# Second expert stage: rows that carry their gates and weights, results added into the output by GpSimd's scatter

## The chip, the cores and the metric

The kernel runs on one core of a Trainium2 chip. The metric is the device time of one execution in microseconds (us), the median of several runs. The engines are named as the profile names them: PE (TensorE matmuls), PEld (its weight loads), DVE (VectorE), ACT (ScalarE), POOL (GpSimd), and SP, which here only issues DMAs.

## The reference, cut to what matters

Two layers follow each other; each is a gated attention and a gated mixture of experts over 4 x 512 tokens of 128 numbers. The change lies in the last part, the experts of layer 1, where every token goes to 2 of 8 experts:

```python
h = _layernorm(x, axis=-1) * (1 + cb) + sb
# _L1_ffn_ref, with x = h as 2048 rows of 128
routing_probs = jax.nn.softmax(x @ gate_w.T, axis=-1)
top_w, top_i = jax.lax.top_k(routing_probs, 2)
top_w = top_w / jnp.sum(top_w, axis=-1, keepdims=True)
gates = jnp.zeros((T, 8)).at[rows, top_i].set(top_w)
out = 0
for e in range(8):
    hid = jax.nn.silu(x @ w1[e].T) * (x @ w3[e].T)      # 448 wide
    out = out + hid @ w2[e].T * gates[:, e:e + 1]
x = x_before + gb * out                                  # gb: one row of 128 for each of the 4 batches
```

## The kernel before

Each engine has a program of its own, written out by hand and executed in order; semaphores join them. `Router` picks the experts and sorts the tokens: it counts how many tokens each expert has, gives each expert as many tiles of 128 rows as it needs (39 tiles for two choices per token), and computes for each tile a column of row numbers, `source` (which token each row is) and `home` (where its result goes). `sources` (L289 to L308) does the last of this on DVE.

`rows_out` (L410) writes the normalised rows to `h_rows` in DRAM, one DMA a batch, on SP. `experts_programs` (L896) then holds the programs of the five engines for the tiles:

- POOL gathers the 128 rows of a tile from `h_rows` into one of four buffers `f_hg` (L978), four tiles ahead, and scatters the results `f_y` of a tile to `back_rows` (L984). A token has two results, each with a row of its own in `back_rows`, and no scatter waits for another. In the loop of POOL, `gather(s + 4)` stands ahead of `scatter(s - 2)`.
- PE transposes the gathered tile (L1154), multiplies it with the expert's two up matrices (16 matmuls, L1167) and with its down matrix (L1180). The order is: transpose of tile s + 1, up of tile s, down of tile s - 1.
- ACT copies the transposed tile (L1095) and one weight matrix (L1111) and takes the silu (L1102). DVE copies the other matrix (L1030), multiplies the two halves (L1042) and copies the result out of PSUM to one of three buffers `f_y` (L1056).
- After the last tile SP waits for all scatters (L961), reads `back_rows` back, a token's two rows side by side (`f_back`, L964). For each of the 16 columns of tokens ACT scales the first result by its weight (L1143), DVE adds the second (L1080), multiplies with the gate `gb` (L1084) and adds x (L1085), and SP stores a batch of the output (L969).

The weights of the two choices are computed by `gates` on DVE (L1016 to L1019) at the start of the tiles, from `r_weight`, which ACT takes with one `exp` (L346).

## Time and profile before

| | us |
|---|---|
| median of 3 runs | 586.7 |
| lowest and highest of them | 586.08, 589.87 |
| span of the profiled execution, first to last instruction | 586.0 |
| PE busy | 526.7 (90%) |
| DVE, ACT, POOL busy | 424.8, 328.6, 315.5 |

The profiled execution has no time of its own beside its span; the span is 0.1 us under the lowest run and 0.7 us under the median. The page's shares are averages over stages with different limits. In the table of stages the tiles of the second experts are the stretch from 457 to 566 us, and what comes after them the stretch from 566 to 586 us.

### The profile page before, as it was taken

How to read it: one execution, taken by the hardware profiler on the slowest of the kernel's cores; microseconds unless marked ns; L12 is line 12 of the kernel's file. 1: busy time of each engine (PE TensorE's matmuls, PEld its weight loads, DVE VectorE, ACT ScalarE, POOL GpSimd, SP SyncE). 2: the span in 40 equal slices, each digit the busy share in tenths (PEclk: the TensorE clock that was granted, in tenths of full speed). 3: DMA queues.
4: the chain of work that ended last, by engine and by line, in shares of the span. 5: the costliest groups of instructions: out<-in, count | busy, mean ns of one | idle time of the engine just before them, and what ended most of it. 6: DMA issues, size and time to landing. Idle time of an engine off the chain costs nothing.

```text
span 586.0 us, 13132 instructions
## 1 busy us (share of the span) xinstructions
PE 526.7 (90%) x4044; PEld 374.2 (64%) x4044; DVE 424.8 (72%) x1662; ACT 328.6 (56%) x544; POOL 315.5 (54%) x478
## 2 busy tenths in 40 slices
PE   5989979967489999999999999999998899999960
PEld 5667769965157445444444454445577799999960
DVE  4776736735859899999999999996678454454436
ACT  3854426632573477777777777776630544444423
POOL 3441154417644486566686668666710677777630
PEclk9999989998699899999999999999999899999995
DMA  8500112221671546647634653433850111111115
GB/s 317 221 2 19 55 35 71 71 70 52 126 145 24 122 104 129 126 108 169 153 88 110 154 135 72 93 91 66 299 151 19 45 48 51 49 49 51 43 37 204
DMA packets 90498, 58.21 MB, mean 99 GB/s; under 512 B 72674, under 2 KB 76771, under 8 KB 88615
## 3 DMA queue, kind: packets, MB, share of 16 engines
q1 hardware_dynamic: 81550, 41.18, 28.0%
q0 software_dynamic: 3744, 7.68, 5.1%
q10 hardware_dynamic: 5136, 8.52, 4.1%
q8 instruction: 35, 0.57, 0.4%
q14 instruction: 33, 0.26, 0.2%
HBM read 37.72 MB, written 19.63 MB: 98 GB/s over the span
## 4 chain that ended last, share of the span: by engine, by line
PE 76%; DVE 12%; DMA 4%; issue 3%; ACT 3%; POOL 2%; SPq 0%; ACTq 0%; POOLq 0%; DVEq 0%
PE banks L1167 15%; PE banks L2021 13%; PE banks L2009 12%; PE banks L1995 11%; PE banks L1180 9%; DVE banks L1718 2%; PE banks L1961 1%; PE banks L1154 1%; PE banks L765 1%; DMA f_hg<-scratch_h_rows,r_source 1%; PE banks L366 1%; DMA a_at<-scratch_back_rows,home 1%; PE banks L2109 1%; DVE f_upd L1080 1%; DVE a_rest_ L1637 1%
## 5 line engine op out<-in xcount | busy, mean ns | idle before, releaser
L1718 DVE CUSTOM_DVE_ANT_1 banks<-banks,a_mask 128x480 f32<-128x480 f32 (+14 forms) x480 | 190.0, 459 | 14.7 <-PE banks L1995 12.9
L1867 ACT ACTIVATE a_prob_<-banks 128x1024 f32<-128x1024 f32 x160 | 154.1, 1021 | 48.7 <-PE banks L2009 48.7
L1534 POOL TENSOR_SCALAR_AFFINE_SELECT a_prob_<-a_prob_ 128x512 f32<-128x512 f32 x128 | 80.8, 635 | 67.0 <-ACT a_prob_ L1867 67.0
L1995 PEld LDWEIGHTS banks<-a_k_u_,a_q_u_ 72*128 72x128 bf16 x512 | 64.9, 148 | 64.5 <-DVE a_neg_max_ L1718 31.1
L1995 PE MATMUL banks<-a_k_u_,a_q_u_ 72*128 72x512 bf16 (+15 forms) x512 | 102.4, 291 | 2.4 <-DVE a_neg_max_ L1718 2.4
L1167 PE MATMUL banks<-f_hgt,f_w_now 128*112 128x128 f32 (+1 forms) x808 | 101.2, 277 | 0.0
L2009 PE MATMUL banks<-a_q_u_,a_k_x_ 75*128 75x512 bf16 x320 | 97.4, 386 | 0.4 <-ACT a_prob_ L1867 0.4
L1167 PEld LDWEIGHTS banks<-f_hgt,f_w_now 128*112 128x112 f32 (+1 forms) x808 | 95.6, 184 | 0.0
L978 POOL DMA_INDIRECT f_hg<-scratch_h_rows,r_source x62 | 59.6, 962 | 61.2 <-DVE r_source L299 31.6
L2021 PE MATMUL banks<-a_prob_,a_v_g_ 128*32 128x512 f32 (+3 forms) x1024 | 83.5, 444 | 0.4 <-POOL a_prob_ L1534 0.4
L1718 DVE DVE_READ_ACCUMULATOR2_ANT a_neg_max_<- 128x1 f32 x512 | 72.3, 143 | 0.0
L1180 PE MATMUL banks<-w,f_hidt 112*128 (+1 forms) x496 | 66.2, 277 | 0.0
L1180 PEld LDWEIGHTS banks<-w,f_hidt 112*128 112x128 f32 (+1 forms) x496 | 60.9, 193 | 0.4 <-issue 0.4
L1111 ACT COPY f_w_now<-w 128x448 f32 (+1 forms) x62 | 31.3, 506 | 41.8 <-issue 22.4
L984 POOL DMA_INDIRECT scratch_back_rows<-f_y,r_home x39 | 38.4, 984 | 27.3 <-DVE f_y L1056 26.9
L1042 DVE TENSOR_TENSOR f_hidt<-banks,f_sil 112x512 f32<-112x512 f32 x39 | 27.0, 692 | 33.6 <-PE banks L1167 28.0
L2021 PEld LDWEIGHTS banks<-a_prob_,a_v_g_ 128*32 128x32 f32 x1024 | 27.1, 110 | 37.0 <-issue 19.7
L1030 DVE COPY f_w_now<-w 128x448 f32 (+1 forms) x62 | 25.9, 418 | 30.7 <-issue 29.7
L1095 ACT COPY f_hgt<-banks 128x128 f32<-128x128 f32 x62 | 16.4, 265 | 52.2 <-PE banks L1154 52.2
L2009 PEld LDWEIGHTS banks<-a_q_u_,a_k_x_ 75*128 75x128 bf16 x320 | 26.6, 102 | 17.0 <-ACT a_prob_ L1867 12.5
L1512 POOL TENSOR_SCALAR a_k_x_<-a_k_u_ 72x512 bf16<-72x512 bf16 x32 | 35.4, 1105 | 0.1
L1878 ACT COPY a_o_sb_<-banks 128x512 f32<-128x512 f32 x32 | 18.7, 585 | 18.7 <-PE banks L2021 18.7
(247 smaller groups left out, 714.1 us busy)
## 6 DMA issues: line engine op xcount, KB each, us to landing
a_q_u_<-scratch_q_parts SPq DMA_DIRECT2D x15, 576.0 KB
scratch_o_rows<-a_o_sb_ ACTq DMA_DIRECT2D x28, 256.0 KB, 2.2
w<-in_w SPq DMA_DIRECT2D x2, 2048.0 KB, 10.5
w<-in_w SPq DMA_DIRECT2D x2, 1792.0 KB, 12.3
scratch_q_parts<-a_part_ SPq DMA_DIRECT2D x24, 128.0 KB
a_k_u_<-scratch_k_parts SPq DMA_DIRECT2D x48, 48.0 KB
f_back<-scratch_back_rows SPq DMA_DIRECT2D x4, 512.0 KB, 4.7
w<-in_w SPq DMA_DIRECT2D x2, 896.0 KB, 19.6
```

What stands on the lines that cost most here:

```text
L978: nc.gpsimd.indirect_dma_start(out=hg[s % AHEAD][:], out_offset=None, in_=h_rows[:, :], in_offset=bass.IndirectOffsetOnAxis(ap=source[:, s ...
L984: nc.gpsimd.indirect_dma_start(out=back_rows[:, :], out_offset=bass.IndirectOffsetOnAxis(ap=home[:, s:s + 1], axis=0), in_=y[s % YR][:], i ...
L1111: nc.scalar.copy(w_now[s % 2][:, 0, :], w_first(e)).then_inc(w_a, 1)
L1167: last = nc.tensor.matmul(PS[0:FC, 4 + 2 * q + n, c * P:(c + 1) * P], w_now[q][:, n, c * FC:(c + 1) * FC], hgt[q][:], start=True, stop=True)
L1180: last = nc.tensor.matmul(PS[:, 2 + q, 0:D], hidt[q][0:FC, c, :], w_down[0:FC, bass.ds(e, 1), c, :].rearrange("p a d -> p (a d)"), start=( ...
L1512: nc.gpsimd.tensor_scalar(k_x[g % RING][0:ROWS, :].rearrange("r (t c) -> r t c", c=CK), k_u[r][:, :, g % 2 * TG:(g % 2 + 1) * TG].rearrang ...
L1534: nc.gpsimd.affine_select(out=block_p, in_=block_p, pattern=[[0, JH], [1, P]], compare_op=ALU.is_ge, fill=0.0, base=0, channel_multiplier= ...
L1718: last = nc.vector.tensor_tensor_reduce(out=found, in0=found, in1=mask[:, :, TG - 4 * (t + 1):], scale=-1.0, scalar=-MASKED, op0=ALU.add, ...
L1867: nc.scalar.activation(prob[g % 2][:, 2 * e:2 * e + 2].rearrange("p s j t c -> p (s j) t c"), PS[:, b0:b0 + 2, :].rearrange("p s (j c t) - ...
L1995: last = nc.tensor.matmul(PS[:, a % 3, off:off + width], queries[:, g % 2, :, t], k_u[r][:, :, g % 2 * TG:g % 2 * TG + 4 * (t + 1)], start ...
L2009: last = nc.tensor.matmul(PS[:, 3 + 2 * ((NE * g + e) % 2) + n, :], k_x[g % RING][0:ROWS + PARTS, kb * P:(kb + 1) * P], queries[:, g % 2, ...
L2021: last = nc.tensor.matmul(PS[32 * j:32 * (j + 1), 7, kb * P:].rearrange("p (q f) -> p q f", f=P), v_g[g % VR][:, kb, :], prob[g % 2][:, FI ...
```

## The change

The second experts no longer keep two results per token apart. The normalised rows go to a wider scratch, `e_rows`, of 258 numbers a row: the row itself, the gate row `gb` of its batch, and the token's two weights. The gate rows are written by four SP DMAs in the attention before (one each at four successive groups), the weights by four DMAs of 8 bytes a row (two on SP, two on ACT), once DVE has computed them in `shares`, which stands between `choose` and `places` of the second half. GpSimd gathers the wide rows into six buffers instead of four; a buffer is now free when its tile's result is out. ACT picks, for each row of a tile, the weight of the choice that the row stands for (`chosen_share`, two one-column instructions a tile). DVE multiplies the result by the weight and the gate as it leaves PSUM. SP fills the output with x before the first scatter; each scatter then adds its 128 rows into the output in DRAM. Since both results of a token go to one row, each scatter waits until the one before it has landed. The read back of `back_rows`, its scaling and adding, and the stores after it are gone. Rows of a tile that stand for no token are added to 128 spare rows behind the output, which the caller cuts off.

```diff
@@ -74,6 +74,7 @@
 AHEAD = 4
 YR = 3
+WIDE = 2 * D + 2
 def most_tiles(choices):
@@ -215,7 +222,8 @@
             if k:
                 ch.link(nc.vector.scalar_tensor_tensor(self.rest[:, t], self.chosen[:, 0, t], MASKED, self.shifted[:, t],
                                                        ALU.mult, ALU.add))
-                ch.link(nc.vector.tensor_reduce(self.second[:, t], self.rest[:, t], AX.X, ALU.max))
+                nc.vector.tensor_reduce(self.second[:, t], self.rest[:, t], AX.X, ALU.max).then_inc(self.second_ready, 1)
+                ve.wait_ge(self.second_ready, half + 1)
                 ch.link(nc.vector.tensor_tensor(self.gap[:, t], self.rest[:, t], wide(self.second[:, t]), ALU.subtract))
                 left = self.gap
             ch.link(nc.vector.scalar_tensor_tensor(self.first[:, t], left[:, t], 0.0, falling, ALU.is_ge, ALU.mult))
@@ -300,11 +308,10 @@
         if K == 1:
             ch.link(nc.vector.scalar_tensor_tensor(self.home[:], self.tile_of[:, 0], float(P), self.slot[:, 1, 0], ALU.mult, ALU.add))
         else:
-            ch.link(nc.vector.scalar_tensor_tensor(self.free[:], found, 0.0, self.sb["spares"][:, self.layer, 0:S], ALU.is_equal,
-                                                   ALU.mult))
-            ch.link(nc.vector.scalar_tensor_tensor(self.free[:], slots[:, 1], 0.0, self.free[:], ALU.is_gt, ALU.add))
-            ch.link(nc.vector.scalar_tensor_tensor(self.free[:], found, 2.0, self.free[:], ALU.mult, ALU.add))
-            ch.link(nc.vector.tensor_scalar(self.home[:], self.free[:], -2.0, None, ALU.add))
+            ch.link(nc.vector.tensor_scalar(self.free[:], found, 0.0, self.sb["spare"][:], ALU.is_equal, ALU.mult))
+            ch.step(nc.vector.scalar_tensor_tensor(self.home[:], self.free[:], -1.0, found, ALU.add, ALU.add))
+            ch.link(nc.vector.tensor_scalar(self.side[:, 1], slots[:, 1], 0.0, None, ALU.is_gt))
+            nc.vector.tensor_scalar(self.side[:, 0], self.side[:, 1], -1.0, 1.0, ALU.mult, ALU.add).then_inc(self.side_ready, 1)
         ve.wait_ge(self.rows_ready, 1)
@@ -339,10 +346,11 @@
                             ).then_inc(self.h_ready, 1)
     def weights(self, ac):
-        ac.wait_ge(self.member_ready, 2)
         if self.K == 1:
+            ac.wait_ge(self.member_ready, 2)
             self.nc.scalar.activation(self.weight[:], self.shifted[:], ACT.Exp).then_inc(self.weight_ready, 1)
         else:
+            ac.wait_ge(self.second_ready, 2)
             self.nc.scalar.activation(self.weight[:, :, 0], self.second[:], ACT.Exp).then_inc(self.weight_ready, 1)
@@ -407,11 +415,34 @@
+    def rows_of(self, b):
+
+        rows = self.dram["e_rows"] if self.layer else self.dram["h_rows"]
+        return rows[b * T:(b + 1) * T, :].rearrange("(p i) d -> p i d", i=NI)
+
     def rows_out(self, sp):
         for b in range(B):
             sp.wait_ge(self.h_ready, b + 1)
-            sp.dma_start(self.dram["h_rows"][b * T:(b + 1) * T, :].rearrange("(p i) d -> p i d", i=NI),
-                         self.h[:, b * NI:(b + 1) * NI, :]).then_inc(self.h_out, 16)
+            sp.dma_start(self.rows_of(b)[:, :, 0:D], self.h[:, b * NI:(b + 1) * NI, :]).then_inc(self.h_out, 16)
+
+    def gate_rows_out(self, sp, b):
+
+        sp.dma_start(self.rows_of(b)[:, :, D:2 * D], self.sb["gates"][:, b, 1, 1, :].unsqueeze(1).to_broadcast([P, NI, D])
+                     ).then_inc(self.h_out, 16)
+
+    def shares(self, ve, ch):
+
+        nc, later = self.nc, self.weight[:, :, 0]
+        ve.wait_ge(self.weight_ready, 1)
+        ch.link(nc.vector.tensor_scalar(self.total[:], later, 1.0, None, ALU.add))
+        ch.link(nc.vector.reciprocal(self.pair[:, :, 0], self.total[:]))
+        nc.vector.tensor_tensor(self.pair[:, :, 1], self.pair[:, :, 0], later, ALU.mult).then_inc(self.pair_ready, 1)
+
+    def shares_out(self, queue, batches):
+
+        queue.wait_ge(self.pair_ready, 1)
+        for b in batches:
+            queue.dma_start(self.rows_of(b)[:, :, 2 * D:2 * D + 2], self.pair[:, b * NI:(b + 1) * NI, :]).then_inc(self.h_out, 16)
 def phase_first(nc, dram, sb, ps, router, q_buffers):
@@ -906,7 +937,8 @@
     S = most_tiles(K)
     x_sb, PS, ident = sb["x"], ps, sb["ident"]
     eid, source, home = router.eid, router.source, router.home
-    h_rows, back_rows = dram["h_rows"], dram["back_rows"]
+    h_rows, back_rows = dram["e_rows" if layer else "h_rows"], dram["back_rows"]
+    ring = AHEAD + 2 if layer else AHEAD
     L = f"{layer}"
     def buf(name, shape, dt=F32):
@@ -915,32 +947,27 @@ experts_programs
...
-    hg = [buf(f"f_hg{q}_", [P, D]) for q in range(AHEAD)]
+    hg = [buf(f"f_hg{q}_", [P, WIDE if layer else D]) for q in range(ring)]
-        back = buf("f_back", [P, NT, K, D])
-        upd = buf("f_upd", [P, NT, D])
+        second_share, share = buf("f_second_share", [P, S]), buf("f_share", [P, S])
+        share_step, share_ready = semaphore("f_share_step"), semaphore("f_share_ready")
-    hg_in = [semaphore(f"f_hg_in{q}_") for q in range(AHEAD)]
+    hg_in = [semaphore(f"f_hg_in{q}_") for q in range(ring)]
...
@@ -957,35 +984,34 @@
                 sp.wait_ge(y_ready, s + 1)
                 sp.dma_start(back_rows[s * P:(s + 1) * P, :], y[s % YR][:]).then_inc(y_out[s % YR], 16)
         else:
+            for b in range(B):
+                sp.dma_start(dram["out"][b * T:(b + 1) * T, :].rearrange("(p i) d -> p i d", i=NI),
+                             x_sb[:, b * NI:(b + 1) * NI, :]).then_inc(out_done, 16)
+            sp.wait_ge(out_done, 16 * B)
             for q in range(YR):
                 sp.wait_ge(y_out[q], 16 * ((S - 1 - q) // YR + 1))
-            for b in range(B):
-                sp.dma_start(back[:, b * NI:(b + 1) * NI, :, :],
-                             back_rows[b * T * K:(b + 1) * T * K, :].rearrange("(p i k) d -> p i k d", p=P, k=K)
-                             ).then_inc(back_in[b], 16)
-            for b in range(B):
-                sp.wait_ge(x_ready, b + 1)
-                sp.dma_start(dram["out"][b].rearrange("(p i) d -> p i d", i=NI),
-                             x_sb[:, b * NI:(b + 1) * NI, :]).then_inc(out_done, 16)
-            sp.wait_ge(out_done, 16 * B)
-
     def gpsimd(gp):
         def gather(s):
-            if s >= AHEAD:
-                gp.wait_ge(hgt_mm, s - AHEAD + 1)
+            if s >= ring:
+                gp.wait_ge(y_ready if layer else hgt_mm, s - ring + 1)
             nc.gpsimd.indirect_dma_start(
-                out=hg[s % AHEAD][:], out_offset=None, in_=h_rows[:, :],
-                in_offset=bass.IndirectOffsetOnAxis(ap=source[:, s:s + 1], axis=0)).then_inc(hg_in[s % AHEAD], 16)
+                out=hg[s % ring][:], out_offset=None, in_=h_rows[:, :],
+                in_offset=bass.IndirectOffsetOnAxis(ap=source[:, s:s + 1], axis=0)).then_inc(hg_in[s % ring], 16)
         def scatter(s):
+
             gp.wait_ge(y_ready, s + 1)
+            if s == 0:
+                gp.wait_ge(out_done, 16 * B)
+            else:
+                gp.wait_ge(y_out[(s - 1) % YR], 16 * ((s - 1) // YR + 1))
             nc.gpsimd.indirect_dma_start(
-                out=back_rows[:, :], out_offset=bass.IndirectOffsetOnAxis(ap=home[:, s:s + 1], axis=0),
-                in_=y[s % YR][:], in_offset=None).then_inc(y_out[s % YR], 16)
-
-        gp.wait_ge(router.h_out, 16 * B)
+                out=dram["out"][:, :], out_offset=bass.IndirectOffsetOnAxis(ap=home[:, s:s + 1], axis=0),
+                in_=y[s % YR][:], in_offset=None, compute_op=ALU.add).then_inc(y_out[s % YR], 16)
+
+        gp.wait_ge(router.h_out, 16 * B * (3 if layer else 1))
         gp.wait_ge(router.rows_ready, 1)
         for s in range(AHEAD):
             gather(s)
@@ -1053,7 +1073,9 @@
             if s >= YR:
                 ve.wait_ge(y_out[s % YR], 16 * (s // YR))
             if layer:
-                nc.vector.tensor_copy(y[s % YR][:], PS[:, 2 + s % 2, 0:D]).then_inc(y_ready, 1)
+                ve.wait_ge(share_ready, s + 1)
+                nc.vector.scalar_tensor_tensor(y[s % YR][:], PS[:, 2 + s % 2, 0:D], share[:, s:s + 1], hg[s % ring][:, D:2 * D],
+                                               ALU.mult, ALU.mult).then_inc(y_ready, 1)
             else:
                 bias = sb["b2"][:, bass.ds(e, 1), :].rearrange("p a d -> p (a d)")
                 nc.vector.tensor_tensor(y[s % YR][:], PS[:, 2 + s % 2, 0:D], bias, ALU.add).then_inc(y_ready, 1)
@@ -1072,20 +1095,6 @@
             before, e = e, after
         result(S - 1, before)
-        for b in range(B if layer else 0):
-            ve.wait_ge(back_in[b], 16)
-            gb = sb["gates"][:, b, layer, 1, :]
-            for t in range(b * NI, (b + 1) * NI):
-                ve.wait_ge(first_choice, t + 1)
-                ch.step(nc.vector.scalar_tensor_tensor(upd[:, t, :], back[:, t, 1, :], gate[:, 1, t:t + 1],
-                                                       upd[:, t, :], ALU.mult, ALU.add))
-            ch.wait()
-            ub, xb = upd[:, b * NI:(b + 1) * NI, :], x_sb[:, b * NI:(b + 1) * NI, :]
-            ch.link(nc.vector.tensor_tensor(ub, ub, gb.unsqueeze(1).to_broadcast([P, NI, D]), ALU.mult))
-            nc.vector.tensor_tensor(xb, xb, ub, ALU.add).then_inc(x_ready, 1)
-        if layer:
-            ve.wait_ge(x_ready, B)
-
     def scalar(ac):
         def rows_t(s):
@@ -1120,6 +1129,17 @@
                 last = nc.scalar.activation(hidt[s % 2][:, c, :], PS[:, 4 + 2 * (s % 2), c * P:(c + 1) * P], ACT.Relu,
                                             bias=sb["b1"][:, bass.ds(e, 1), c])
             last.then_inc(low_ready, 1)
+
+        def chosen_share(s):
+
+            row = hg[s % ring]
+            if s == 0:
+                ac.wait_ge(router.side_ready, 1)
+            nc.scalar.activation(second_share[:, s:s + 1], row[:, 2 * D + 1:2 * D + 2], ACT.Copy, scale=router.side[:, 1, s:s + 1]
+                                 ).then_inc(share_step, 1)
+            ac.wait_ge(share_step, s + 1)
+            nc.scalar.activation(share[:, s:s + 1], row[:, 2 * D:2 * D + 1], ACT.Identity, scale=router.side[:, 0, s:s + 1],
+                                 bias=second_share[:, s:s + 1]).then_inc(share_ready, 1)
         ac.wait_ge(sb["experts_in"][layer], 16 * sb["experts_loads"][layer])
         ac.wait_ge(eid_ready, 1)
@@ -1131,27 +1151,20 @@
                 after = weights(s + 1)
             if layer:
                 gated(s)
+                chosen_share(s)
             else:
                 biased(s, e)
             e = after
-        if K == 2:
-            ac.wait_ge(gate_ready, 1)
-            for b in range(B):
-                ac.wait_ge(back_in[b], 16)
-                for t in range(b * NI, (b + 1) * NI):
-                    nc.scalar.activation(upd[:, t, :], back[:, t, 0, :], ACT.Copy, scale=gate[:, 0, t:t + 1]
-                                         ).then_inc(first_choice, 1)
-
...
@@ -1476,6 +1489,8 @@
                         factors_out(b)
                     if at_step == NORM_AT + 2:
                         factors_in(b)
+                if GROUPS - 8 <= g < GROUPS - 4:
+                    router.gate_rows_out(sp, g - (GROUPS - 8))
                 if g == GROUPS - 3:
                     gather_sums(B - 1)
                     gather_outputs(B - 1)
@@ -1491,6 +1506,7 @@
                 sp.dma_start(sb["w_down"][1][0:F1 // 4, half * (E // 2):(half + 1) * (E // 2)],
                              dram["w2_1"][:, half * (E // 2):(half + 1) * (E // 2)]).then_inc(loaded, 16)
             router.rows_out(sp)
+            router.shares_out(sp, (0, 1))
             experts_sync(sp)
         @block.gpsimd
@@ -1818,6 +1834,7 @@
             router.shared_tail(ve)
             router.positions(ve, ch, 0)
             router.choose(ve, ch, 1)
+            router.shares(ve, ch)
             router.places(ve, ch, 1)
             router.positions(ve, ch, 1)
             router.bases(ve, ch)
@@ -1934,6 +1951,7 @@
             router.modulate(ac, B - 1)
             router.rows_back(ac, B - 1)
             router.weights(ac)
+            router.shares_out(ac, (2, 3))
             experts_scalar(ac)
         @block.tensor
...
-    "h_rows": (B * T, D), "back_rows": (2 * B * T + most_tiles(2) * P, D),
+    "h_rows": (B * T, D), "e_rows": (B * T, WIDE), "back_rows": (most_tiles(1) * P, D),
...
-    dram["out"] = nc.dram_tensor("out", (B, T, D), F32, kind="ExternalOutput").ap()
+    dram["out"] = nc.dram_tensor("out", (B * T + P, D), F32, kind="ExternalOutput").ap()
-    return result.results[0]["out"]
+    return result.results[0]["out"][0:B * T].reshape(B, T, D)
```

POOL in the second experts, around the middle tiles, before. The semaphores reuse names of the first phase: `rope_in` counts the transposes of PE, `silu_done` the finished results.

```order
L978 DMA f_hg1_1<-scratch_h_rows,r_source1 128x128 [waits rope_in]
L984 DMA scratch_back_rows<-f_y0_1,r_home1 9088x128 [waits silu_done]
L978 DMA f_hg2_1<-scratch_h_rows,r_source1 128x128 [waits rope_in]
L984 DMA scratch_back_rows<-f_y1_1,r_home1 9088x128 [waits silu_done]
L978 DMA f_hg3_1<-scratch_h_rows,r_source1 128x128 [waits rope_in]
```

The same place now; `spread_mm` counts the finished results, and `const_in`, `squares_in` and `attn_in` are the landings of the three buffers of results.

```order
L999 DMA f_hg3_1<-scratch_e_rows,r_source1 128x258 [waits spread_mm]
L1010 DMA out<-f_y0_1,r_home1 2176x128 [waits squares_in,spread_mm]
L999 DMA f_hg4_1<-scratch_e_rows,r_source1 128x258 [waits spread_mm]
L1010 DMA out<-f_y1_1,r_home1 2176x128 [waits attn_in,spread_mm]
L999 DMA f_hg5_1<-scratch_e_rows,r_source1 128x258 [waits spread_mm]
```

The two kinds still alternate; the gather now waits for a result instead of a transpose, and each scatter has a second wait, for the landing of the scatter before it.

DVE in the router, where `choose` ends and `places` begins, before (`r_both` is the set of both choices, `r_own` a choice's ranks):

```order
L223 TENSOR_TENSOR r_chosen<-r_first,r_lead 128x64 [waits ht_ready]
L229 TENSOR_TENSOR r_both<-r_chosen 128x64 [waits ht_ready]
L238 TENSOR_TENSOR r_own<-banks,r_chosen 128x64 [waits r_ranks_mm0,r_member_ready0]
L238 TENSOR_TENSOR r_own<-banks,r_chosen 128x64
L240 TENSOR_REDUCE r_pos_f<-r_own 128x2x8 [waits ht_ready]
```

The same place now, with `r_pair` for the two weights:

```order
L231 TENSOR_TENSOR r_chosen<-r_first,r_lead 128x64 [waits ht_ready]
L237 TENSOR_TENSOR r_both<-r_chosen 128x64 [waits ht_ready]
L437 TENSOR_SCALAR r_total<-r_weight 128x16 [waits r_weight_ready0]
L438 RECIPROCAL r_pair<-r_total 128x16 [waits ht_ready]
L439 TENSOR_TENSOR r_pair<-r_pair,r_weight 128x16 [waits ht_ready]
L246 TENSOR_TENSOR r_own<-banks,r_chosen 128x64 [waits r_ranks_mm0,r_member_ready0]
```

Three instructions that stood at the start of the tiles (with a fourth, a copy, that is gone) now stand ahead of `r_own`.

## Rows read from the trace of the kernel before

**Rows 1.** The page: the span.

```profile
span 586.0 us, 13132 instructions
```

**Rows 2.** Busy time by stage: us, engines with instruction counts, granted clock, DMA.

```profile
152.00:200.00 48.00, 41.80 (x206) 25.02 (x210) 38.49 (x164) 25.23 (x36) 22.03 (x38) 0.89 0.51 106
200.00:420.00 220.00, 218.71 (x1801) 108.74 (x1794) 200.32 (x946) 164.06 (x183) 150.41 (x288) 1.00 0.50 121
...
457.00:566.00 109.00, 108.75 (x971) 108.59 (x972) 52.91 (x114) 52.65 (x117) 71.21 (x73) 0.98 0.17 46
566.00:586.00 20.00, 0.56 (x6) 0.37 (x4) 10.12 (x25) 5.06 (x16) 1.94 (x2) 0.62 0.44 164
```

**Rows 3.** The chain that ended last, its end: start us, us, what.

```profile
566.04 0.97 POOL scratch_back_rows L984
...
567.31 2.27 DMA scratch_back_rows<-f_y,r_home
...
569.65 3.23 DMA f_back<-scratch_back_rows
...
573.49 1.16 DVE f_upd L1080 x4
...
582.90 0.69 DVE x_sb L1085
```

**Rows 4.** The chain that ended last, amid the tiles (one tile of 39).

```profile
491.26 0.11 PE banks L1154
491.37 1.75 PE banks L1167 x16
493.12 0.89 PE banks L1180 x8
```

**Rows 5.** Timeline of POOL amid the tiles: start us, us, engine, line, idle before.

```profile
480.87 0.98 POOL L984 DMA_INDIRECT scratch_back_rows<-f_y,r_home  x1 [0.49 <-DVE f_y L1056]
482.16 0.97 POOL L978 DMA_INDIRECT f_hg<-scratch_h_rows,r_source  x1 [0.30 <-issue]
483.62 0.99 POOL L984 DMA_INDIRECT scratch_back_rows<-f_y,r_home  x1 [0.49 <-DVE f_y L1056]
```

**Rows 6.** Timeline of DVE: the first result, and two amid the tiles.

```profile
463.79 0.29 DVE L1056 COPY f_y<-banks 128x128 f32<-128x128 f32 x1 [0.20 <-PE banks L1180]
...
480.30 0.29 DVE L1056 COPY f_y<-banks 128x128 f32<-128x128 f32 x1 [0.15 <-PE banks L1180]
```

**Rows 7.** The scatter's line L984, 455 to 566 us: issue to landing.

```profile
DMA to landing us min/median/max: 2.2/2.3/3.9
```

**Rows 8.** The gather's line L978, 460 to 566 us: issue to landing.

```profile
DMA to landing us min/median/max: 2.4/2.6/3.6
```

**Rows 9.** DMA queue of POOL, 450 to 572 us: packets, MB, share of 16 engines.

```profile
q0 software_dynamic: 2496, 5.12, 15.3%
```

**Rows 10.** Waits from 455 to 572 us: total us, times, longest.

```profile
ACT f_hgt L1095 <- PE banks L1154: 40.2, 38, 2.0
```

**Rows 11.** The chain that ended last, where the tiles begin.

```profile
452.26 0.19 DVE r_source L299
...
454.64 2.57 DMA f_hg<-scratch_h_rows,r_source
```

**Rows 12.** Timeline of the router's end and the tiles' start, DVE and ACT.

```profile
441.43 0.23 ACT L346 ACTIVATE r_weight<-r_second 128x16 f32<-128x16 f32 x1 [1.99 <-DVE r_both L229]
...
441.95 0.35 DVE L238 TENSOR_TENSOR r_own<-banks,r_chosen 128x64 f32<-128x64 f32 x2 [0.55 <-PE banks L390]
...
454.45 0.17 DVE L1016 TENSOR_SCALAR f_total<-r_weight 128x16 f32<-128x16 f32 x1
...
455.16 0.42 DVE L1019 COPY f_gate<-f_total 128x16 f32<-128x16 f32 x1
```

**Rows 13.** DMA queue of SP, 300 to 400 us: packets, MB, share of 16 engines.

```profile
q1 hardware_dynamic: 19914, 6.64, 32.2%
```

**Rows 14.** The store of the output, line L969, on SP: issue to landing.

```profile
DMA to landing us min/median/max: 2.0/2.0/2.0
```

More of the change, by code:

```diff
@@ L191, in __init__ @@
              "ranks_mm", "one_hot_ready", "slots_mm", "rows_ready", "weight_ready"))
+        if K == 2:
+            self.side_ready, self.second_ready, self.pair_ready = (semaphore(n) for n in ("side_ready", "second_ready", "pair_ready"))
     def shared_tail(self, ve):
@@ L494, in _ @@
             sp.dma_start(squares_f[:], dram["squares"]).then_inc(squares_in, 16)
-            for name in ("falling", "table", "router", "tokens", "spares"):
+            for name in ("falling", "table", "router", "tokens", "spare"):
                 sp.dma_start(sb[name][:], dram[name]).then_inc(small_in, 16)
@@ L941, in experts_programs @@
     sb["y_out"] = [(y_out[q], 16 * ((S - 1 - q) // YR + 1)) for q in range(YR)]
-    back_in = [semaphore(f"f_back_in{b}_") for b in range(B)] if layer else None
     def w_first(e):
@@ L1063, in vector @@
         weights(0, e)
-        gates()
+        if not layer:
+            gates()
         for s in range(S):
@@ L1149, in rows_t @@
         def rows_t(s):
-            pe.wait_ge(hg_in[s % AHEAD], 16 * (s // AHEAD + 1))
+            pe.wait_ge(hg_in[s % ring], 16 * (s // ring + 1))
             if s >= 2:
                 pe.wait_ge(hgt_ready, s - 1)
-            nc.tensor.transpose(PS[:, s % 2, 0:P], hg[s % AHEAD][:], ident[:]).then_inc(hgt_mm, 1)
+            nc.tensor.transpose(PS[:, s % 2, 0:P], hg[s % ring][:, 0:D], ident[:]).then_inc(hgt_mm, 1)
         def up(s):
```

30 lines of the change are left out of this document (12 added, 18 removed).

## The prediction

> **What bounds the kernel now.** I read the table of stages first. From 457 to 566 us the second experts keep PE busy for 108.75 of 109 us; from 566 to 586 us PE does 0.56 us of work [rows 2]. The change touches these two stretches. The chain of waits then says what each is made of. Amid the tiles it is PE alone, 0.11 + 1.75 + 0.89 = 2.75 us a tile [rows 4]. In the end piece it is a line of hand-overs: last scatter 2.27 us, read back 3.23 us, four batches on DVE until 583.6 us, and a store that lands 2.0 us after its issue [rows 3, 14]; with the span at 586.0 [rows 1] some 0.4 us follow the last landing. Third, POOL amid the tiles: a scatter of 0.98 us, a gap of 0.30, a gather of 0.97, then 0.49 us of idling until the next result [rows 5]. So POOL fills 2.26 of 2.75 us: not the bound, but near it. Last, how long its transfers take from the start of the issue: a scatter 2.3 us, a gather 2.6 us, both medians [rows 7, 8]. Before, nobody amid the tiles waits for a scatter's landing; now the next scatter does.
>
> **What goes.** Everything between the last scatter's landing, 567.31 + 2.27 = 569.6 us [rows 3], and the end: 586.0 - 569.6 = 16.4 us, less the 0.4 us after a landing, is 16.0 us.
>
> **What comes amid the tiles: a chain of 39 scatters.** A scatter starts when the one before has landed and POOL has woken. POOL starts a scatter 0.28 us after the result it waits for (480.59 to 480.87) [rows 5, 6], and I take that for a landing too. With L from the start of the issue to the landing, a link takes L + 0.28 us. The gather between two scatters is hidden: scatter, gap, gather and gap are 0.98 + 0.30 + 0.97 + 0.30 = 2.55 us, within the link. So the tiles take the longer of 2.75 us (PE) and L + 0.28 us each. With the plain scatter's 2.3 us a link is 2.58 us and PE still decides, by 0.17 us. Everything hangs on how much longer an adding scatter takes than a plain one.
>
> The trace has no adding DMA, so I bound it. From below: a plain scatter, L = 2.3 us. From above: a gather and then a scatter with one issue between them, 2.6 + 2.3 - 0.97 = 3.9 us. What it must do more than a plain scatter is read the old rows from DRAM. A gather, which reads DRAM, lands 0.3 us later than a scatter, which reads SBUF; that is one term. The second reading also occupies the DMA engines: POOL's queue took 15.3% of 122 us for 78 transfers [rows 9], 0.24 us each, and I add that once. POOL has more to describe: between nothing and half of 0.97 us more; I take 0.17 us, a third of that half. Together 0.3 + 0.24 + 0.17 = 0.7 us: **L = 3.0 us, a link of 3.28 us.** It is nearer to the plain scatter than to the upper end because reading and writing of different rows can overlap.
>
> The Trainium skill speaks against the change here: "Collectives: The Full Stack", the section on the bandwidth ceiling, says that an add in the DMA costs no time in its adder, but needs two source reads per chunk on one ring, and so halves the rate. By that the term of 0.24 us would be all that is added, an estimate of 2.54 us for L, and PE and the chain would be nearly level; no run here shows it.
>
> **The start of the chain.** The first result is ready at 463.79 + 0.29 = 464.08 us [rows 6]. In POOL's order a gather stands ahead of the first scatter, and it now waits for this very result: 0.28 + 0.97 + 0.30 later, at 465.63 us, the first scatter starts. To this come delays ahead of the tiles. DVE's three instructions of `shares`: 0.71 us from the first to the one behind them; 0.55 us of that fit into the idle time before `r_own`, so 0.16 us [rows 12]. The `exp` they need took 0.23 us on an ACT that had idled 1.99 us [rows 12], and it now waits for a result five DVE instructions earlier; nothing. The gather of rows twice as long: its 0.24 us once more, on the path, since the first tiles wait for the gather (2.57 us) [rows 11]. Together 0.4 us.
>
> **The sum.** First scatter 465.63 + 0.4, then 38 links, one landing and 0.4 us to the end: 466.4 + 38 (L + 0.28) + L = 466.15 + 39 T, with T = L + 0.28. For T = 3.28 that is 594.1 us of span. Against 586.0: the tail gives 16.0 us back; the chain takes 39 x 0.53 = 20.7; 0.4 at the start and some 3.0 by which the last scatter trails the last result are the rest. The median stands 0.7 us over this span and the lowest run 0.1; I add 0.4: **594.5 us**.
>
> **What costs nothing, and its cover.** ACT's two one-column instructions a tile are priced by the 128x16 `exp`: 2 x 0.23 us; before the copy of the transposed tile ACT waits 40.2 us in 38 waits for PE [rows 10], 1.06 us each. Without that cover a tile would grow by 0.5 us. DVE's multiplication replaces a copy of 0.29 us; four such operations took 1.16 us [rows 3], the same. The gather starts 1.4 us later in its tile's cycle, since it waits for a result; three tiles, 8.2 us, still lie between it and the transpose that needs it, and it takes under 3. The eight-byte weights are 2048 pieces, 128 for each of 16 DMA engines. SP's queue took 32.2% of 100 us for 19914 packets [rows 13], 26 ns each: 3.3 us, and 2.0 us to land, from about 442.7 us until 448 us, while the first gather cannot start before `source` is done at 452.45 us [rows 11]; 4 us of cover, and past it every microsecond counts. The rows in pieces of 512 bytes and the store of x (2.0 us a batch [rows 14]) lie in the same gap. The gate rows add 1 MB to a stretch where PE is busy 218.71 of 220 us at a DMA share of 0.50 [rows 2]; SP's four issues delay loads that are made ahead. If the chain makes PE idle a sixth of the time, its granted clock may fall, as to 0.89 where it was busy 41.80 of 48 us [rows 2]; 2.75 / 0.89 = 3.09 us a tile stays under 3.28.
>
> **The rivals.** (1) Faster: the adding scatter lands within 2.47 us, the link stays under 2.75, and PE keeps the period. Then the last two scatters decide: 566.04 + 0.4, one link of 2.58, 2.3 to land, 0.4 to the end, and up to 0.5 for the lag of the chain behind the gathers: 572.2, as a run 572.5 us. For it: reading old rows for all 128 at once could hide in the 0.97 us of issue. Against it: the gather's 0.3 us. Chance 0.17. The Trainium skill's fit for POOL's transfers, "DMA: Bandwidth & Descriptors", in the anatomy of one DMA, is 2.0 us plus the bytes at 436 GB/s, whatever the operation: by it 64 KB need an estimate of 2.15 us and this rival holds. The trace has 2.3 and 2.6 us for the same bytes, so the direction, which that fit leaves out, matters already.
> (2) The chain decides but gives back less than the tail is worth. It is level with before at T = (586.0 - 466.15) / 39 = 3.07, L = 2.79 us. L from 2.64 to 2.94 us ends within 1%, 580 to 592 us: chance 0.25. L from 2.47 to 2.64, 574 to 580 us: 0.10.
> (3) The forecast, L over 2.94 us: 0.48, of which 0.1 past 3.4 us (610 us), where issue and reading follow each other with no overlap.
> (4) The chain is not the bound and something ahead of the tiles is: the weights land late and the first gather waits. To cancel the tail it would need 14 us, four times what the weights take. Inside the range; as a cause of its own no chance above 0.02, counted with (3). That the chain doesn't exist is excluded by the order: each scatter has the second wait.
>
> **The numbers.** About 1% is what a measurement of this kernel can tell from no change, 5.9 us, or 0.15 us of a link. Faster by more than 1%: (1) and the lower part of (2), 0.27. Within 1%: 0.25. Slower: 0.48. The range reaches from rival (1), 571.5, to L = 3.4 us, 610 us: about 0.05 is left out below and 0.1 above. The likeliest case's own range is 592 to 610.
>
> **What will show it.** The scatter's time to landing: about 3.0 us, against 2.3. POOL's longest wait amid the tiles is for a landing in `out`, not for `f_y`. From about the seventh tile on, DVE's write of `f_y` waits for a free buffer (a scatter then lags by the 3 us that three buffers give) and PE has a gap of half a microsecond in every tile. After the last result only about three scatters follow, 5 to 8 us, and no DVE work. I am wrong if POOL waits for `f_y` as before and the tiles stay at 2.75 us: then the adding is hidden, and the time is near 572. I am also wrong if the first gather starts later than 453.5 us.

## The result, and the profile after

| | before | the changed kernel |
|---|---|---|
| median, us | 586.9 (4 runs beside it) | 635.6 (4 runs) |
| lowest and highest, us | 586.08, 589.87 | 635.35, 636.25 |
| span of the profiled execution, us | 586.0 | 633.8 (its own run: 635.59) |

The ratio is 1.0823, with a 95% interval from 1.0797 to 1.085: 8% slower, 48.6 us. The prediction had the direction, slower, and a chain of scatters as the cause; its 594.5 us is 41 us short, and the time lies beyond the range's upper end of 610 us.

The table of stages of the changed kernel (columns as in [rows 2]; the second stretch is longer):

```profile
457.00:566.00 109.00, 88.67 (x716) 85.53 (x714) 37.69 (x82) 56.47 (x146) 64.90 (x52) 0.94 0.29 49
566.00:634.00 68.00, 31.96 (x258) 30.24 (x257) 15.13 (x34) 18.34 (x48) 31.53 (x23) 0.80 0.24 33
```

PE, which had 108.75 of 109 us in [rows 2], has 88.67 and does 258 of its instructions after 566 us. It waits for others now. The view of the scatter's line (count, duration in ns, min/median/max, first and last start), with what POOL waited for before it (us, times), and the time to landing:

```profile
L1010 POOL DMA_INDIRECT out<-f_y,r_home x39: 1549/1586/1632, 464.9 to 625.0; - x39
...
  DVE f_y L1077: 52.1, 35
  DMA out<-f_y,r_home: 6.3, 3
...
DMA to landing us min/median/max: 3.2/3.3/4.8
```

The line above it, the wait for the landing, is an instruction of its own in POOL's queue; the wait for the result has none:

```profile
L1009 POOLq EVENT_SEMAPHORE  x38: 17/17/17, 468.2 to 624.2; - x38
```

The scatter's issue takes 1.59 us where [rows 5] have 0.98, the landing 3.3 us where [rows 7] have 2.3. POOL's timeline amid the tiles (columns as in [rows 5]) shows the pace:

```profile
515.92 1.59 POOL L1010 DMA_INDIRECT out<-f_y,r_home  x1 [1.20 <-DVE f_y L1077]
517.81 0.99 POOL L999 DMA_INDIRECT f_hg<-scratch_e_rows,r_source  x1 [0.30 <-issue]
519.91 1.59 POOL L1010 DMA_INDIRECT out<-f_y,r_home  x1 [1.11 <-DVE f_y L1077]
...
524.03 1.59 POOL L1010 DMA_INDIRECT out<-f_y,r_home  x1 [1.23 <-DVE f_y L1077]
```

A link takes 3.99 to 4.12 us here; over all, (624.97 - 464.86) / 38 = 4.21. The end of the chain of waits (start us, us, what) tells what a link is made of:

```profile
612.66 3.40 DMA out<-f_y,r_home
616.06 0.04 DVEq L1076
616.10 0.04 issue
616.14 0.36 DVE f_y L1077
616.50 0.31 issue
616.82 3.30 DMA out<-f_y,r_home
620.11 0.03 issue
620.14 0.02 POOLq L1009
620.15 0.81 issue
620.96 3.26 DMA out<-f_y,r_home
624.22 0.02 issue
624.25 0.02 POOLq L1009
624.26 0.49 issue
624.75 1.77 POOLq L1247
```

From a landing (620.11) to the next scatter's start (620.96) pass 0.85 us, while no result is missing any more. The `f_y` that the page names before a scatter is not the result that this scatter sends: here it is the last of all, written when the landing at 616.06 has freed its buffer, while the scatter at 616.82 is the third from the end. After the last scatter comes no DVE and no read back, but this instruction, which closes POOL's own queue:

```profile
L1247 POOLq DRAIN  x1: 8868/8868/8868, 624.7 to 624.7; - x1
```

The program ends at 633.8 us, 0.2 us after this instruction and some 5.6 us after the last landing at 624.97 + 3.2 us.

### The profile page after: what moved, and what is told of

Same layout as the page of the kernel before. It is cut to its first block, busy times and chain, and to the rows that moved or that the text cites. A ratio compares the mean times of both kernels' runs of the same rounds, so it can differ in the third digit from the quotient of the medians.

```text
span 633.8 us, 13210 instructions
## 1 busy us (share of the span) xinstructions
PE 537.4 (85%) x4044; PEld 380.7 (60%) x4044; DVE 413.1 (65%) x1637; ACT 346.1 (55%) x606; POOL 340.1 (54%) x478
## 3 DMA queue, kind: packets, MB, share of 16 engines
q0 software_dynamic: 8736, 10.27, 9.4%
## 4 chain that ended last, share of the span: by engine, by line
PE 59%; DMA 12%; DVE 12%; issue 10%; POOL 3%; ACT 2%; POOLq 0%; SPq 0%; ACTq 0%; DVEq 0%
PE banks L2039 12%; PE banks L2027 11%; PE banks L2013 10%; PE banks L1180 7%; DMA out<-f_y,r_home 7%; PE banks L1193 5%; DMA f_hg<-scratch_e_rows,r_source 4%; DVE banks L1734 2%; POOL out L1010 2%; DVE f_y L1077 1%; PE banks L1979 1%; PE banks L796 1%; PE banks L1167 1%; PE banks L374 1%; DMA a_at<-scratch_back_rows,home 1%
## 5 line engine op out<-in xcount | busy, mean ns | idle before, releaser
L1180 PE MATMUL banks<-f_hgt,f_w_now 128*112 128x128 f32 (+1 forms) x808 | 107.3, 288 | 0.0
L1180 PEld LDWEIGHTS banks<-f_hgt,f_w_now 128*112 128x112 f32 (+1 forms) x808 | 101.0, 193 | 0.0
L1010 POOL DMA_INDIRECT out<-f_y,r_home x39 | 61.7, 1583 | 58.7 <-DVE f_y L1077 52.1
L1077 DVE SCALAR_TENSOR_TENSOR f_y<-banks,f_share,f_hg 128x128 f32<-128x128 f32 x39 | 13.7, 351 | 82.4 <-issue 52.8
L999 POOL DMA_INDIRECT f_hg<-scratch_e_rows,r_source x39 | 38.8, 994 | 34.3 <-DVE r_source L307 19.0
L1167 PE MATMUL banks<-ident,f_hg 128*128 128x128 f32 x62 | 19.0, 306 | 37.2 <-DMA f_hg<-scratch_e_rows,r_source 33.4
L999 POOL DMA_INDIRECT f_hg<-scratch_h_rows,r_source x23 | 22.0, 956 | 30.0 <-PE banks L1167 15.5
## 6 DMA issues: line engine op xcount, KB each, us to landing
a_q_u_<-scratch_q_parts SPq DMA_DIRECT2D x15, 576.0 KB
```

The costliest lines, as they stand in the source:

```text
L999: nc.gpsimd.indirect_dma_start(out=hg[s % ring][:], out_offset=None, in_=h_rows[:, :], in_offset=bass.IndirectOffsetOnAxis(ap=source[:, s: ...
L1010: nc.gpsimd.indirect_dma_start(out=dram["out"][:, :], out_offset=bass.IndirectOffsetOnAxis(ap=home[:, s:s + 1], axis=0), in_=y[s % YR][:], ...
L1180: last = nc.tensor.matmul(PS[0:FC, 4 + 2 * q + n, c * P:(c + 1) * P], w_now[q][:, n, c * FC:(c + 1) * FC], hgt[q][:], start=True, stop=True)
```

## The experiments

The kernel before was timed in the same jobs: 586.97 us (15 runs; e1 to e3), 586.21 us (11 runs; e4 to e7), 587.73 us (7 runs; e8 and e9). Theory A, from reading the two traces: a link is 3.3 us of landing and 0.8 us of waking (from the landing to the next scatter's start), and the waking is long because the wait for the landing is an instruction of its own in POOL's queue, while the wait for the result rides on the DMA. Theory B: POOL simply needs that long after a landing, whichever wait it is.

**e1: the two waits in the other order.**

```diff
         def scatter(s):
-            gp.wait_ge(y_ready, s + 1)
             if s == 0:
                 gp.wait_ge(out_done, 16 * B)
             else:
                 gp.wait_ge(y_out[(s - 1) % YR], 16 * ((s - 1) // YR + 1))
+            gp.wait_ge(y_ready, s + 1)
             nc.gpsimd.indirect_dma_start(
```

> The changed kernel with the two waits of a scatter in the other order, so that the wait for the landing of the scatter before rides on the DMA instruction and the wait for the result stands alone. Theory A (a wait that stands alone ahead of POOL's DMA instruction costs 0.8 us from release to start, one that the DMA instruction carries 0.3 us): the link falls from 4.1 to 3.3 + 0.33 = 3.63 us, 38 links give 18 us back, the run takes 613 to 618 us. Theory B (POOL wakes that late after any DMA landing): the link stays at 4.1 us and the run at 635 us.

615.88 us (612.54 to 617.77, 5 runs), ratio 1.0499 [1.0471, 1.0527]. In e1 the instruction of its own is the wait for the result (L1009 there), and POOL's timeline is:

```profile
L1009 POOLq EVENT_SEMAPHORE  x39: 17/17/17, 462.4 to 598.3; - x39
...
500.84 1.59 POOL L1010 DMA_INDIRECT out<-f_y,r_home  x1 [0.69 <-DMA out<-f_y,r_home]
502.73 0.99 POOL L999 DMA_INDIRECT f_hg<-scratch_e_rows,r_source  x1 [0.30 <-issue]
504.39 1.59 POOL L1010 DMA_INDIRECT out<-f_y,r_home  x1 [0.66 <-DMA out<-f_y,r_home]
```

A link is 3.55 us here (3.63 over all) with the landing still at 3.3: the waking is 0.25 us instead of 0.8. Two swapped lines give back 20 us, and the releaser before the scatter is now the landing (32.1 us in 35 waits). Theory A holds. In the changed kernel the same idle time stands under `f_y`: the wait that ends last is not the one that is named there.

**e2: a plain chain.** The scatter doesn't add, but waits as in the changed kernel.

```diff
-                in_=y[s % YR][:], in_offset=None, compute_op=ALU.add).then_inc(y_out[s % YR], 16)
+                in_=y[s % YR][:], in_offset=None).then_inc(y_out[s % YR], 16)
```

> The changed kernel with the adding taken out of the scatters (each overwrites its rows in the output, so one result of each token and x are lost); the chain of waits stays as it is. Theory A (the adding costs 0.6 us of issue and 0.4 us behind it): issue 0.98 us, landing 2.3 us, link 2.3 + 0.8 = 3.1 us, first scatter at 465 and 38 links and the end: 592 to 597 us. Rival (the landing in the output, or being chained, is what takes 3.3 us, not the adding): landing stays at 3.3 us and the run near 635 us.

597.29 us (595.64 to 598.93, 2 runs), ratio 1.0182 [1.0136, 1.0229]; the median lies 0.3 us above the range expected. Of the scatter of e2:

```profile
L1010 POOL DMA_INDIRECT out<-f_y,r_home x39: 971/988/1177, 463.6 to 584.9; - x39
...
DMA to landing us min/median/max: 2.2/2.3/3.6
```

As theory A has it, links are 3.05 us (499.87, 502.92), 2.3 of landing and 0.75 of waking. The adding costs 1.0 us of landing, of which 0.6 us are POOL's longer issue and 0.4 lie behind it.

**e2b: both edits.** Plain chain, swapped waits.

> Plain overwriting scatters (as in the run before this one) and the two waits in the other order: 2.3 + 0.33 = 2.63 us a link, under PE's 2.75, so PE keeps the period as in the kernel before, and the last scatter starts near 568 us. If POOL's end of program takes 8.8 us from the start of its last DMA (8.7 to 8.8 us in both traces so far, hidden in the kernel before), the span is 577 us; if only the landing counts, 571 us. Theory B (late waking after a landing): 2.3 + 0.8, 592 us or more.

583.85 us (580.83 to 587.25, 8 runs), ratio 0.9938 [0.9911, 0.9964], span 582.8. Its last scatters follow each other in 2.5 us:

```profile
566.31 0.98 POOL L1010 DMA_INDIRECT out<-f_y,r_home  x1 [1.54 <-DMA out<-f_y,r_home]
568.82 0.97 POOL L1010 DMA_INDIRECT out<-f_y,r_home  x1 [1.53 <-DMA out<-f_y,r_home]
571.32 0.97 POOL L1010 DMA_INDIRECT out<-f_y,r_home  x1 [1.54 <-DMA out<-f_y,r_home]
573.81 0.97 POOL L1010 DMA_INDIRECT out<-f_y,r_home  x1 [1.53 <-DMA out<-f_y,r_home]
```

PE is busy for 108.63 of 109 us from 457 to 566 us, as before. So with a link shorter than PE's 2.75 us the mechanism of the first rival is there, but my time for it is missed by 6 us: the last scatter starts at 573.8, not 568. A few landings are late (4.57, 4.12, 4.24 and 3.94 us from one scatter to the next), and a link of 2.56 us gives back only 0.2 us per tile.

**e3: two targets.** Even tiles are added into the output, odd tiles into a second one that SP fills with x, and each scatter waits, in e1's order, for the one two before it.

```diff
-                gp.wait_ge(y_out[(s - 1) % YR], 16 * ((s - 1) // YR + 1))
+                gp.wait_ge(y_out[(s - 2) % YR], 16 * ((s - 2) // YR + 1))
...
-                out=dram["out"][:, :], ...
+                out=(dram["odd"] if s % 2 else dram["out"])[:, :], ...
```

> Adding scatters, but even tiles add to the output and odd tiles to a second array filled with x, so a scatter waits only for the one two before it (the odd tiles' results are missing in the output). If only the chain binds, the tiles go back to PE's 2.75 us and the run takes 578 us. Theory A says that POOL's own work binds next: 1.58 + 0.30 + 0.99 + 0.30 = 3.17 us a tile for 33 tiles with a gather, last scatter near 580 to 585 us, with the end 589 to 594 us. If the DMA engines were the limit of the adding, the landing would grow past 3.3 us and the run would stay above 600 us.

589.54 us (588.04 to 590.42, 4 runs), ratio 1.0047 [1.0021, 1.0073]. POOL's timeline of e3:

```profile
500.62 1.59 POOL L1012 DMA_INDIRECT scratch_odd<-f_y,r_home  x1 [0.30 <-issue]
502.51 0.99 POOL L1001 DMA_INDIRECT f_hg<-scratch_e_rows,r_source  x1 [0.31 <-issue]
503.81 1.59 POOL L1012 DMA_INDIRECT out<-f_y,r_home  x1 [0.30 <-issue]
```

No wait is left, and still a tile takes 1.59 + 0.30 + 0.99 + 0.31 = 3.19 us: POOL's issuing is itself longer than PE's 2.75 us. As long as POOL also issues the gathers, a better order of waits cannot make the adding as cheap as before.

**e4: six result buffers** (`YR = 6` for 3).

> The changed kernel with six result buffers instead of three (YR = 6). Theory: the chain of adding scatters sets the end by itself (39 links of 4.1 to 4.2 us from the first result on); DVE's waits for a free buffer and PE's gaps are only its echo. The results are then ready earlier, by three tiles of lag, but no scatter starts earlier: 633 to 637 us, no difference from the changed kernel, with the last scatter starting at 624 to 626 us and PE done some 10 to 13 us earlier. Rival: three buffers make PE idle, and PE's stalls lengthen the kernel; then six give back a good part of what the stalls cost, and the time falls under 630 us.

635.48 us (2 runs), ratio 1.0833 [1.0803, 1.0864], last scatter at 624.87: the buffers cost nothing, and the chain sets the end. One number of mine failed: PE ends only 1.8 us earlier, not 10 to 13. With six buffers PE waits for gathers as much as before (36.7 us in 28 waits; 33.4 in 23), since in POOL's program a gather stands behind a scatter that waits. POOL's waits for `f_y` shrink from 52.1 to 17.1 us and those for the landing grow from 6.3 to 40.2, at nearly the same pace (4.19 us a link for 4.21): again the name was not the cause.

**e5: one late gather on POOL, in the kernel before.**

```diff
             scatter(S - 1)
+            gp.wait_ge(x_ready, B)
+            nc.gpsimd.indirect_dma_start(
+                out=hg[0][:], out_offset=None, in_=h_rows[:, :],
+                in_offset=bass.IndirectOffsetOnAxis(ap=source[:, 0:1], axis=0)).then_inc(hg_in[0], 16)
```

> The kernel before, with one more gather on POOL that is issued only when DVE has finished the last batch of the output (about 583.6 us); SP waits for its landing too, and nothing reads it. Theory (after its last DMA, POOL's queue needs some 9 us to close, whatever has landed): POOL's last DMA starts at about 583.9 us and the span ends about 8.9 us after its issue, 592 to 594 us, some 7 us over the kernel before. Rival (the program ends with the last landing): the gather lands 2.6 us after its issue, 586.5 us, and the span is 586.5 to 587.5 us, at most 1 us over the kernel before.

594.09 us (593.37 to 594.56, 4 runs), ratio 1.0129 [1.0105, 1.0152]. In e5, and in the kernel before:

```profile
L1239 POOLq DRAIN  x1: 9050/9050/9050, 582.6 to 582.6; - x1
...
L1239 SPq DRAIN  x1: 7/7/7, 585.6 to 585.6; - x1
```

```profile
L1234 POOLq DRAIN  x1: 9098/9098/9098, 566.9 to 566.9; - x1
```

The late gather starts at 582.82; SP, which waits for its landing, is done at 585.6; POOL's drain lasts until 591.6 and the span ends at 591.9. In the kernel before, the same 9.1 us began at 566.9 us and ended at 576.0, under the tail.

**e6: the weights without the adding.** Wide rows, shares and the multiplication on DVE as in the changed kernel, but plain scatters into `back_rows`, where each result has its own row and no scatter waits for another. At the end SP reads the rows back and DVE adds:

```diff
+        for b in range(B if layer else 0):
+            ve.wait_ge(back_in[b], 16)
+            both, xb = back[:, b * NI:(b + 1) * NI], x_sb[:, b * NI:(b + 1) * NI, :]
+            ch.link(nc.vector.tensor_tensor(xb, xb, both[:, :, 0, :], ALU.add))
+            nc.vector.tensor_tensor(xb, xb, both[:, :, 1, :], ALU.add).then_inc(x_ready, 1)
```

> A mixture: wide rows, the weights and the multiplication on DVE as in the changed kernel, but each result goes by a plain scatter, which waits for no other, to a row of its own, as in the kernel before; at the end the two rows of a token are read back and DVE adds both to x (two additions of some 0.7 us per batch, no ACT). The wait for the row numbers rides on the first gather instead of standing alone. Theory (the adding and the chain cost everything, the weights and the multiplication amid the tiles cost nothing): POOL's last scatter lands at 568 to 570 us as before, then 3.2 us of reading, four times 1.4 us on DVE, 2.0 us for the store and 0.4: a span of 579 to 582 us, 5 us under the kernel before; a ratio of 0.985 to 0.995. Rival (the weights or the wide rows delay the tiles too): the last scatter lands after 572 us and the span is 584 us or more.

581.66 us (580.23 to 583.35, 6 runs), ratio 0.9912 [0.989, 0.9934], against 1.0823 for the changed kernel: it beats both, and the span of 580.8 us lies in the expected 579 to 582. The stages of e6, and its tail on POOL and DVE:

```profile
457.00:566.00 109.00, 108.76 (x971) 108.40 (x970) 55.01 (x115) 74.37 (x194) 71.15 (x74) 0.98 0.24 68
```

```profile
566.56 0.97 POOL L1017 DMA_INDIRECT scratch_back_rows<-f_y,r_home  x1 [0.31 <-issue]
...
572.23 0.69 DVE L1108 TENSOR_TENSOR x_sb<-x_sb,f_back 128x512 f32<-128x512 f32 x1 [6.08 <-DMA f_back<-scratch_back_rows]
...
577.66 0.69 DVE L1109 TENSOR_TENSOR x_sb<-x_sb,f_back 128x512 f32<-128x512 f32 x1
```

PE is busy for 108.76 of 109 us although ACT has gone from 52.65 us [rows 2] to 74.37: picking the weights and multiplying cost nothing amid the tiles. From the last scatter's landing (566.56 + 2.25 = 568.8) to the end at 580.8 it takes 12.0 us, against 16.4 before.

**e7: half of each row.** Each adding scatter carries 64 of the 128 columns.

> The changed kernel, in which each adding scatter carries 64 of the 128 columns, so half the bytes in as many rows, to a target of its own; the output is left with x alone, and the results are missing from it. Theory: POOL's longer issue (1.59 against 0.98 us) goes by rows, not by bytes: it stays at 1.5 to 1.6 us, the landing falls from 3.3 to about 3.2 us, links stay at 4.0 to 4.1 us, and the span is 627 to 634 us. Rival (issue and landing go by bytes): issue 1.0 to 1.3 us, landing 2.6 to 2.8 us, links of 3.5 us, a span of 605 to 615 us.

629.80 us (629.07 to 630.53, 2 runs), ratio 1.0737 [1.0705, 1.0768]. The scatter of e7:

```profile
L1012 POOL DMA_INDIRECT scratch_half<-f_y,r_home x39: 1549/1586/1631, 466.6 to 619.9; - x39
...
DMA to landing us min/median/max: 3.0/3.2/4.2
```

The issue is the same 1.59 us, the landing 0.1 us shorter: the price of adding does not go by bytes. That it goes by rows fits the packets, but no run varied the rows. The queues' lines (packets, MB, share) of the changed kernel, of e2b and of e7 say the same:

```profile
q0 software_dynamic: 8736, 10.27, 9.4%
```

```profile
q0 software_dynamic: 4368, 10.27, 6.7%
```

```profile
q0 software_dynamic: 8736, 8.99, 8.5%
```

The adding makes (8736 - 4368) / 39 = 112 more packets per scatter, however many bytes they carry.

**e8 and e9: more code.** In the changed kernel the links over 4.5 us (4.62, 5.41, 5.59, 4.71) each hold a packet of 16 KB in the queue of instructions q8. To see whether loading code makes landings late, SP executes 120 waits per tile that are already fulfilled, in the changed kernel (e8) and in e2b (e9):

```diff
             sp.wait_ge(out_done, 16 * B)
+            for s in range(S):
+                for _ in range(120):
+                    sp.wait_ge(y_ready, s + 1)
```

> The changed kernel, in which SP, idle during the tiles, executes 120 waits per tile that are already fulfilled (on the count of finished results): 4680 more instructions of 64 bytes, 0.30 MB more code to load during the tiles. In the changed kernel the trace has 9 packets of 16 KB in the instruction queue q8 during 38 links; the four links over 4.5 us (4.62, 5.41, 5.59, 4.71) all hold one, and no link without one is over 4.21 us. Theory (a packet of code that comes among those of a scatter makes its landing late): q8 or q14 has some 18 more packets of 16 KB, or twice as many of 8 KB, amid the tiles, more links are over 4.5 us (7 to 12 instead of 4), the mean link grows by 0.1 to 0.3 us and the span by 4 to 12 us, 637 to 646 us. Rival (the coincidence with code is chance): as many slow links as before and a span within 2 us of 633.8.

> The same 120 fulfilled waits per tile on SP, in the kernel with the plain chain and the swapped waits (no adding; the output is overwritten, so x and one of a token's results are missing), where a link has no slack: 2.56 us, and the links over 3 us (3.23, 4.57, 4.12, 4.24, 3.94) all hold one of the 9 packets of the instruction queue q8. Theory: more packets of code, 10 to 14 links over 3 us instead of 5 or 6, the last scatter starts at 578 to 590 us instead of 573.8 and the span is 587 to 599 us. Rival (chance): 5 or 6 slow links, the last scatter at 572 to 575 us, a span of 581 to 584 us.

687.99 us (ratio 1.1721 [1.1692, 1.1749]) and 666.53 us (1.1349 [1.1319, 1.1378]). The edit did less and cost more than meant. The traces hold 2339 of these instructions, not 4680, and only from 536.5 us on in e8 and from 516.3 us in e9, so the later half of each chain alone ran beside them. SP itself became the end: its last of these waits starts at 684.6 us in e8, and both expected spans are missed. What the runs can tell stands in the chain, whose last scatter starts at 624.86 us in e8 (624.97 without) and at 574.25 us in e9 (573.81). The additional code came through the other queue; the lines of the changed kernel and of e8, of the whole program:

```profile
q8 instruction: 35, 0.57, 0.4%
q14 instruction: 34, 0.28, 0.1%
```

```profile
q8 instruction: 35, 0.57, 0.4%
q14 instruction: 52, 0.43, 0.2%
```

About three times as many packets in q14 beside the later half of the chain (16 for 5 in e8; 12 for 5 in e9) move its end by 0.5 us at most. In e8, as in the changed kernel, four of the nine links that hold a packet of q8 are over 4.5 us (4.97, 5.26, 5.45, 5.47), and none of the others is over 4.21. e9 is less clear: eight links are over 3 us, where e2b has five and the theory wanted 10 to 14; three of the eight hold no packet of q8, and two of these three one of q14. So late landings mostly come with q8; that q8 causes them is not shown, since its packets stayed as they were.

## Why the prediction was wrong

**What held.** POOL's chain of landings took PE's place as the bound, the kernel became slower, and the levels were ordered as worked out: a plain chain with a short waking stays under PE's 2.75 us where no landing is late (2.56 us in e2b), an adding one doesn't. The adding scatter's 3.3 us lie between my bounds of 2.3 and 3.9. The first scatter, expected at 466.0 us, starts at 464.86; the attention ended 1.2 us earlier in this execution (first gather at 452.01 for 453.22). The start's 0.4 us came true, but by luck: DVE's `shares`, put at 0.16, cost nothing (the second half of `choose` starts 1.21 us earlier than before, at 437.16, and `source` 1.22 us earlier, at 451.04), while the wider gather, put at 0.24, cost 0.41 (2.98 us to land for 2.57). The weights arrive in time: in all twelve traces the first gather starts 0.3 to 0.8 us after `source`, at 450.7 to 453.7 us, so rival (4) is out. ACT's and DVE's new work is hidden (e6). DVE's waits ahead of `f_y` came (52.8 us in 21 waits without a named releaser, 16.7 us in 7 for a landing), and PE's gaps with them; three scatters followed the last result, with no DVE work behind it, as foretold, but the last landing came 11.7 us after that result, not 5 to 8.

**What failed**, against the sum's 594.1 us of span, 39.7 us in all:

| step | predicted | measured | us |
|---|---|---|---|
| start | first scatter 466.0 | 464.86 | -1.2 |
| "POOL starts a scatter 0.28 us after the result it waits for, and I take that for a landing too" | 0.28 a link | 0.80 | 38 x 0.52 = +19.8 |
| L, its issue term above all | 3.0 | 3.3 | 38 x 0.3 = +11.4 |
| (no step) late landings | 0 | mean link 4.213, less 4.10 | 38 x 0.113 = +4.3 |
| "0.4 us after a landing" at the end | L + 0.4 = 3.4 | 8.83 | +5.4 |

The largest failure is the waking. A price read at one wait was carried to another that the order of waits treats differently. The `order` rows showed both waits at one DMA; which of them would be an instruction of its own they don't show. The trace of before did hold such a case. Ahead of the first gather, two waits follow each other in the code (for the rows and for the row numbers), and the chain there has

```profile
452.48 0.02 POOLq L989
452.49 0.73 issue
```

between `source` being done and the gather's start: a standing wait and 0.73 us behind it, half a microsecond dearer than the 0.28 us of [rows 5, 6]. I had the place in [rows 11] and read on past it. e6, where those two waits are swapped, starts the gather 0.28 us after `source`.

Of L, the terms for reading and packets, 0.3 + 0.24 us, came to 0.4; the term for POOL's issue, 0.17, to 0.61. The upper bound for it, half of 0.97 us, was too low: I reasoned that only a part of the descriptors would be added, and the adding needs 112 packets per scatter more. "Perfetto Trace Analysis" of the Trainium skill, its section "DMA Instruction — SWDGE (GPSIMD)", has the profile's end of such an instruction where the last descriptor is written. e7 fits that: with half the bytes and as many packets the issue stays the same. The two rules of the Trainium skill that the prediction weighed gave estimates of 2.54 and 2.15 us for L; the trace has 3.3. "Collectives: The Full Stack" of the Trainium skill, in the section on the bandwidth ceiling, counts the second read and a descriptor for it, and gives no time for writing that descriptor. The fit in "DMA: Bandwidth & Descriptors" of the Trainium skill, in the anatomy of one DMA, has no term for adding. By that fit half the bytes are worth an estimate of 0.08 us; e7's landing is 0.1 us shorter.

The end failed because I took the 0.4 us after a landing from a tail under which POOL's 9.1 us of draining were hidden. When the change made POOL's last DMA the last thing of all, the cover was gone; I had asked that question of the work amid the tiles and not of the program's end.

The signal I named, POOL's longest wait for a landing rather than for `f_y`, came out as its opposite on the page (52.1 against 6.3 us), with the mechanism right. Read alone, that row denies the chain; only the pace of 4.1 us, and e1 and e4, tell that the landing was it. I also asked for about 3 us of lag and half a microsecond of PE gap per tile. The gap is 4.1 - 2.75 = 1.4 us, since the link is longer. The lag is 8.5 us (the last result is ready at 616.5 and its scatter starts at 624.97): three buffers hold a result for two links and a waking, and the result takes 0.44 us of that (616.06 to 616.50), so even L = 3.0 us would have given 2 x 3.28 + 0.28 - 0.44 = 6.4.

## What to carry to other kernels

Before a transfer that nobody waited for becomes a link of a chain, price the whole link: issue, landing, and the waking of the engine by that very wait, which was 0.25 or 0.8 us depending on whether the wait rides on the DMA or stands alone; put the wait that ends last where it rides. Ask also what ends the program when the tail goes: a GpSimd queue that issues DMAs to the last costs its 9 us of draining in the open. Where a change has several parts, try them apart: here the weighting without the adding gained 4.5 us (half a microsecond of it, by the trace, from a swapped wait), and with the adding and its chain the kernel lost 48.6.

## What the runs showed of the hardware that was not expected

- GpSimd's issue of an adding scatter of 128 rows takes 1.59 us, of a plain one 0.98, and with half the bytes the adding one still takes 1.59.
- A wait of its own ahead of a POOL DMA adds 0.5 us when it is the one that ends last: links of 4.1 and 3.55 us (adding), 3.05 and 2.56 us (plain), with nothing but the two waits swapped.
- The DRAIN that closes POOL's queue took 8.87 to 9.12 us in all twelve traces, from about its last DMA on, though the last landing comes within 2.3 to 3.3 us of the issue.
- Single landings are late, by up to 1.5 us in the changed kernel and 2.0 us in e2b. In seven of the eight traces with the chain, no link without a packet of the instruction queue q8 is more than 0.2 us over the median link; in the eighth, e9, three are. Why is open.
